# Front joined, side work reordered, and three products of the second scan made token-major and turned by TensorE

## The reference

```python
xs = _clamp(_layernorm(xs, norm_w, norm_b))
xz = xs @ in_proj_w.T
xin, z = jnp.split(xz, 2, axis=-1)
xc = silu(conv4(xin) + conv_b)               # 4 taps along the tokens
dt = softplus(xc @ x_proj_dt @ dt_proj_w.T + dt_proj_b); B, C = xc @ x_proj_bc
h = exp(dt * A) * h + (dt * x) * B           # 16 states, one step per token
y = einsum(h, C) + xc * D
out = layernorm(clamp((y * silu(z)) @ out_proj_w.T))
```

## Time and profile before

| | us |
|---|---|
| Median of 3 runs (203.24 to 204.24) | 203.94 |
| The profiled execution | 204.56 |
| Its span, first to last instruction | 202.8 |
| Around the span | 1.76 |

### The profile page before, as it was taken

The page is one execution under the profiler, slowest core; times in us unless marked ns, Lnnn a source line. Parts: engine busy times, 40 slices in busy tenths (PEclk is TensorE's granted clock), DMA queues, the critical chain, the costliest instruction groups (busy, mean ns, idle before and its releaser), DMA issues. The chain is left out here.

```text
span 202.8 us, 3714 instructions
## 1 busy us (share of the span) xinstructions
PE 178.0 (88%) x1194; PEld 149.2 (74%) x1194; DVE 135.2 (67%) x316; ACT 122.5 (60%) x281; POOL 106.5 (53%) x140
## 2 busy tenths in 40 slices
PE   6999858996887377799989999999989999999993
PEld 5678644643253124489979999899989999999992
DVE  2485999999899869998663727581377573333333
ACT  2717998999563636336658566767554655555530
POOL 4500044679796688689483445544466344344400
PEclk9999999999999969999999999999999999999999
DMA  5960299998450000000000000000000000000000
GB/s 148 327 194 0 36 389 353 326 306 255 170 216 36 0 0 0 0 0 3 2 0 3 2 0 3 0 0 3 0 2 0 3 2 0 22 9 3 0 0 26
DMA packets 7234, 14.38 MB, mean 71 GB/s; under 512 B 513, under 2 KB 3113, under 8 KB 6961
## 3 DMA queue, kind: packets, MB, share of 16 engines
q1 hardware_dynamic: 7216, 14.17, 21.8%
HBM read 13.88 MB, written 0.29 MB: 70 GB/s over the span
## 5 line engine op out<-in xcount | busy, mean ns | idle before, releaser
L933 DVE SCALAR_TENSOR_TENSOR acc<-dbx_ps,comb,acc 128x128 f32<-128x128 f32 x96 | 28.9, 344 | 30.8 <-PE dbx_ps L1211 30.5
L345 POOL TENSOR_TENSOR hc<-hs,cb 128x1024 f32<-128x1024 f32 x15 | 35.4, 2357 | 24.5 <-DMA cb<-c_rows 12.5
L1183 PE MATMUL bc_ps<-x_hi,w_hi 128*128 128x256 f32 x128 | 41.6, 325 | 0.8 <-DVE dbx_ps L767 0.8
L618 ACT ACTIVATE hid<-bc_ps,par 128x256 f32<-128x256 f32 x64 | 26.8, 471 | 21.9 <-PE bc_ps L1185 21.7
L363 POOL TENSOR_TENSOR w_lo<-w1b,w_hi 128x256 fp32r<-128x256 f32 x32 | 23.5, 735 | 27.4 <-ACT w_hi L610 27.2
L777 DVE TENSOR_TENSOR_SCAN hs<-da,dbx_ps 128x1024 f32<-128x1024 f32 x16 | 36.4, 2278 | 0.1
L1185 PE MATMUL bc_ps<-x_hi,w_lo 128*128 128x256 f32 x128 | 36.1, 282 | 0.0
L1184 PE MATMUL bc_ps<-x_lo,w_hi 128*128 128x256 f32 x128 | 35.9, 280 | 0.0
L1211 PE MATMUL dbx_ps<-w2b,hid 128*128 128x128 f32 (+1 forms) x256 | 33.9, 277 | 0.8 <-DVE acc L933 0.8
L1211 PE MATMUL dbx_ps<-w2a,hid 128*128 128x128 f32 x256 | 34.1, 276 | 0.3 <-ACT hid L618 0.2
L621 ACT ACTIVATE hid<-bc_ps 128x512 f32<-128x512 f32 x32 | 19.1, 597 | 24.0 <-PE bc_ps L1185 23.9
(11 more groups left out here) (183 smaller groups left out, 233.7 us busy)
## 6 DMA issues: line engine op xcount, KB each, us to landing
w1a<-w_in SPq DMA_DIRECT2D x2, 1024.0 KB, 9.1
cb<-c_rows SPq DMA_DIRECT2D x2, 1024.0 KB, 6.3
w1b<-w_in SPq DMA_DIRECT2D x2, 1024.0 KB, 14.4
cb<-c_rows SPq DMA_DIRECT2D x2, 768.0 KB, 5.4
cb<-taps_in SPq DMA_DIRECT2D x1, 512.0 KB, 5.1
cb<-c_rows SPq DMA_DIRECT2D x2, 256.0 KB, 3.9
par<-packed_in SPq DMA_DIRECT2D x1, 473.0 KB, 4.0
x_cm<-x_in SPq DMA_DIRECT2D x2, 128.0 KB, 2.1
```

Of the source, the lines that this page charges most:

```text
L345: nc.gpsimd.tensor_tensor(hc[p][:], hs[p][:], cb[:, k].rearrange("p i (o t) -> p i o t", o=1).to_broadcast([128, PAIR, DC, T]), ALU.mult). ...
L618: ins = nc.scalar.activation(hid[p][:, c, :], h_ps[p][:, T * c:T * (c + 1)], ACT.Gelu, bias=par[:, bass.ds(u * UC + at, 1)])
L933: nc.vector.scalar_tensor_tensor(acc[k][:, t, :], o_ps[:, w // span % RING, 128 * t:128 * (t + 1)], comb[layer][b][:, t, bass.ds(u, 1)], a ...
L1183: nc.tensor.matmul(h_ps[p][:, T * c:T * (c + 1)], w1_hi[w][:, at], x_hi[b][:], start=True, stop=False)
```

## The change

It has four parts.

1. The front. The taps are read from SBUF, without the ScalarE copies, and made in halves; ScalarE's copy of x comes ahead of its other work; TensorE's idle products are 256 wide and wait for nothing but their operands.
2. Softplus. One table set holds both Exp and Ln, so the loads around Ln go; the logarithm of 1 that this table gives is subtracted. ScalarE copies the C rows and B columns of batch 0, which VectorE did; GpSimd takes two subtractions of batch 0. For batch 1 ScalarE makes 1+e and VectorE is left with one instruction of two.
3. Side work. `step_x` follows `step_1` on GpSimd; the four high parts of the weights come between the scans, the low parts one by one; GpSimd does root_3 ahead of `hc` of m = 9.
4. Products. For m = 11, 13 and 15 (TURNED) VectorE's product goes. TensorE turns dt*x of batch 1 to token-major once (`turn`), ScalarE copies it to SBUF and scales it per token by a column of B (`token_products`, four instructions a pair), and TensorE turns the result into `dbx` (`turned_product`, eight transposes a pair). The `spread_b` of these pairs goes too.

```diff
...
+TURNED = (NP + 3, NP + 5, NP + 7)
...
+        dbx_tok = [sb(f"dbx_tok_{p}", [128, PAIR, TT, DI]) for p in range(RING)]
...
+        plan = [("constants",), ("x_stats", 0), ("x_stats", 1), ("x_norm", 0), ("rows_out",),
+                ("inner_x", 0), ("taps", 0, 0), ("in_proj", 0), ("taps", 0, 1), ("taps", 1), ("x_norm", 1), ("conv", 0), ("conv", 1), ("v", 0),
                 ("inner_x", 1), ("in_proj", 1), ("v_end",), ("bc", 0), ("softplus", 0), ("first_rows",), ("conv1", 0),
...
         b1_in = {3: [("silu1",)], 5: [("softplus", 1), ("bc_copy", 1)]}
-        b1_out = {1: [("z", 1)], 2: [("v", 1)], 3: [("bc", 1)], 4: [("rounding",), ("step_1",)], 5: [("step_x",)]}
+        b1_out = {1: [("z", 1)], 2: [("v", 1)], 3: [("bc", 1)], 4: [("rounding",), ("step_1",), ("step_x",)]}
         for k in range(NP):
             plan += [("pair_in", 0, k)] + b1_in.get(k, []) + [("pair_out", 0, k)] + b1_out.get(k, [])
+            if k == NP - 2:
+                plan += [("stage_lo", 0)]
+        plan += [("stage", u) for u in range(STAGED)]
         for k in range(NP):
             plan += [("pair_in", 1, k)] + [(name, 0, 0) for name in before_states.get(k, [])]
-            if k in (0, 2):
-                plan += [("stage", k), ("stage", k + 1)]
+            if k == 0:
+                plan += [("stage_lo", 1), ("stage_lo", 2)]
+            if k == 1:
+                plan += [("stage_lo", 3)]
+            if k in (0, 1, 3):
+                plan += [("tokens", TURNED[min(k, 2)])]
             if k == NP - 1:
                 plan += [("experts", 0, 0, 0, 1), ("bias2", 0, 0), ("experts", 0, 0, 1, 2)]
             plan += [("pair_out", 1, k)] + [(name, 0, 0) for name in after_states.get(k, [])]
...
+                for c in range(DC):
+                    low, e = dt_a[0][:, c], dt_e[0][:, c]
+                    pool.wait_ge(s["one_e"], c + 1)
+                    nc.gpsimd.tensor_tensor(low, e, low, ALU.subtract).then_inc(s["low_done"], 1)
...
+            def in_time(work):
+                at, root = work.index(("pair_out", 1, 1)), work.index(("root_3", 0, 0))
+                return work[:at] + [work[root]] + work[at:root] + work[root + 1:]
+            for step, *arg in in_time(plan):
...
                 act.wait_ge(s["ident_ready"], 1)
                 for c in range(DC):
                     ins = nc.scalar.activation(diag_d[:, c, :], ident[:], ACT.Identity, scale=col("d_skip")[:, c:c + 1])
@@ -459,10 +491,7 @@
             def rows_out():
                 act.wait_ge(s["wv_ps"], 1)
                 nc.scalar.activation(w_dt[:], halves(wv_ps), ACT.Copy).then_inc(s["wv_ready"], 1)
-            def taps_in(c):
-                act.wait_ge(s["taps_loaded"], 16)
-                nc.scalar.activation(taps_ps[c], taps_sb[:, c, :], ACT.Copy).then_inc(s["taps_ps"], 1)
+                skip_rows()
...
-                    nc.scalar.preload_act_table_set("exp_and_others")
+                    nc.scalar.preload_act_table_set("natural_log_exp_and_others")
...
-                    nc.scalar.preload_act_table_set("natural_log")
+                        if c == 0:
+                            act.wait_ge(s["ones_ready"], 1)
+                            nc.scalar.activation(ln_one[:], ones[:, 0:1], ACT.Ln).then_inc(s["ln_one_ready"], 1)
                     for c in range(DC):
                         act.wait_ge(s["exp_dt"], c + 1)
                         nc.scalar.activation(dt_l[0][:, c], dt_e[0][:, c], ACT.Ln, bias=ones[:, 0:1]).then_inc(s["ln_dt"], 1)
-                    nc.scalar.preload_act_table_set("exp_and_others")
+                        if c == 0:
+                            act.wait_ge(s["bct_ps"], 1)
+                            nc.scalar.activation(c_row[:, 0, :], bct_ps[0][0:NS, T:2 * T], ACT.Copy).then_inc(s["c_row_ready"], 1)
+                    act.wait_ge(s["ln_one_ready"], 1)
+                    nc.scalar.activation(ln_neg[:], ln_one[:], ACT.Copy, scale=-1.0).then_inc(s["ln_neg_ready"], 1)
+                    nc.scalar.activation(b_tok[:, 0], bct_ps[0][:, 0:TT * NS].rearrange("p (t r) -> p t r", t=TT),
+                                         ACT.Copy).then_inc(s["bct_ready"], 1)
...
-                nc.scalar.preload_act_table_set("natural_log")
                 act.wait_ge(s["exp_dt"], DC + 1)
-                nc.scalar.activation(dt_l[1][:], dt_e[1][:], ACT.Ln, bias=ones[:, 0:1]).then_inc(s["ln_dt"], 1)
-                nc.scalar.preload_act_table_set("exp_and_others")
+                nc.scalar.activation(halves(f_ps), dt_e[1][:], ACT.Identity, bias=ones[:, 0:1]).then_inc(s["one_e1"], 1)
+                nc.scalar.activation(dt_a[1][:], dt_e[1][:], ACT.Ln, bias=ones[:, 0:1]).then_inc(s["ln_raw"], 1)
+                act.wait_ge(s["ln_raw"], 1)
+                act.wait_ge(s["ln_neg_ready"], 1)
+                nc.scalar.activation(dt_l[1][:], dt_a[1][:], ACT.Identity, bias=ln_neg[:, 0:1]).then_inc(s["ln_dt"], 1)
...
+            def token_products(m):
+                j = TURNED.index(m)
+                if j >= RING:
+                    act.wait_ge(s["dbx_pe"], j - RING + 1)
+                for i in range(PAIR):
+                    for t in range(TT):
+                        n = PAIR * (m % NP) + i
+                        ins = nc.scalar.activation(dbx_tok[j % RING][:, i, t, :], dtx_tok[:, t, :], ACT.Identity,
+                                                   scale=b_tok[:, m // NP, t, n:n + 1])
+                ins.then_inc(s["dbx_tok_ready"], 1)
             def pair_in(b, k):
                 for j in (range(AHEAD) if b and k == 0 else (k + AHEAD - 1,) if b else (k,)):
                     if j < NP:
                         decays(b, j, (j + NP * b) % AHEAD)
+                if (b, k) == (1, 0):
+                    act.wait_ge(s["turn_ps"], 1)
+                    nc.scalar.activation(dtx_tok, f_ps.rearrange("p (t d) -> p t d", t=TT), ACT.Copy).then_inc(s["turned"], 1)
+                    act.wait_ge(s["turned"], 1)
...
-            def taps(c):
...
-                dve.wait_ge(s["taps_ps"], c + 1)
+                dve.wait_ge(s["taps_loaded"], 16)
+                at = slice(0, TAPS) if half is None else slice(TAPS // 2 * half, TAPS // 2 * (half + 1))
                 w_in = col("in_w")[:, 128 * c:128 * (c + 1)].rearrange("p (o d) -> p o d", o=1)
-                nc.vector.tensor_tensor(w_tap[:, c], w_in.to_broadcast([C, TAPS, 128]),
-                                        taps_ps[c].rearrange("p (k d) -> p k d", k=TAPS), ALU.mult).then_inc(s["taps_ready"], 1)
+                nc.vector.tensor_tensor(w_tap[:, c, at], w_in.to_broadcast([C, at.stop - at.start, 128]),
+                                        taps_sb[:, c, :].rearrange("p (k d) -> p k d", k=TAPS)[:, at], ALU.mult).then_inc(s["taps_ready"], 1)
...
-                    g, low, e = dt_q[0][:, c], dt_a[0][:, c], dt_e[0][:, c]
                     dve.wait_ge(s["abs_done"], c + 1)
-                    nc.vector.tensor_scalar(g, dt0_ps[c][:, 0:T], col("dt_b")[:, c:c + 1], 0.0, ALU.add, ALU.max).then_inc(s["r_done"], 1)
+                    nc.vector.tensor_scalar(dt_q[0][:, c], dt0_ps[c][:, 0:T], col("dt_b")[:, c:c + 1], 0.0, ALU.add,
+                                            ALU.max).then_inc(s["r_done"], 1)
                     dve.wait_ge(s["exp_dt"], c + 1)
-                    dve.wait_ge(s["r_done"], c + 1)
-                    nc.vector.tensor_tensor(g, g, e, ALU.add)
-                    link(nc.vector.tensor_scalar(low, e, 1.0, 1.0, ALU.add, ALU.subtract))
-                    link(nc.vector.tensor_tensor(g, g, low, ALU.subtract))
-                    if c == 0:
-                        bc_copy()
+                    nc.vector.tensor_scalar(dt_a[0][:, c], dt_e[0][:, c], 1.0, 1.0, ALU.add, ALU.subtract).then_inc(s["one_e"], 1)
                 for c in range(DC):
-                    dve.wait_ge(s["ln_dt"], c + 1)
-                    nc.vector.tensor_tensor(dt[:, c, 0, :], dt_q[0][:, c], dt_l[0][:, c], ALU.add).then_inc(s["dt0_ready"], 1)
+                    with_log(c)
+                    with_low(c)
...
-                dve.wait_ge(s["exp_dt"], DC + 1)
-                dve.wait_ge(s["relu_done"], 1)
-                link(nc.vector.tensor_scalar(halves(f_ps), dt_e[1][:], 1.0, 1.0, ALU.add, ALU.subtract))
-                nc.vector.tensor_tensor(dt_q[1][:], halves(f_ps), dt_e[1][:], ALU.subtract).then_inc(s["rounded"], 1)
+                dve.wait_ge(s["one_e1"], 1)
+                nc.vector.scalar_tensor_tensor(dt_q[1][:], halves(f_ps), 1.0, dt_e[1][:],
+                                               ALU.subtract, ALU.subtract).then_inc(s["rounded"], 1)
...
+                if m in TURNED:
+                    dve.wait_ge(s["dbx_pe"], TURNED.index(m) + 1)
+                else:
+                    dve.wait_ge(s["dbx_done"], made(m) + (1 + RING))
...
-                if 1 < m < NB * NP:
+                if 1 < m < NB * NP and m not in TURNED:
                     inputs(m // NP, m % NP, m % RING)
...
```

(47 more changed lines are left out.)

53 lines of the change are left out of this document (30 added, 23 removed).

## The result

| | before | after |
|---|---|---|
| Median of 10 runs each, one chip | 204.86 (203.24 to 206.23) | 202.62 (201.93 to 203.29) |
| Profiled execution | 204.56 | 202.17 |
| Its span | 202.8 | 200.4 |

The ratio is 0.990 (95% interval 0.9867 to 0.9933): 1.0% or 2.0 us faster, where I forecast 3.4 of 203.94 us, 1.7%. The profiles differ by 2.4 us.

What follows compares the result with a forecast made beforehand. VectorE was taken to set the time to about 87 us, TensorE from the experts' first output on. Gains 1.1+0.85+0.95-0.65+1.75-1.0+0.4 = 3.4 bring the median from 203.94 to 200.5 us; range 198.6 to 202.7.

Steps and rivals of the forecast that it cites:

- no low granted clock past 76: Sign from TensorE: the forecast would be wrong if its granted clock was low past 76 us.
- no idle time before gate_out: Sign between the scans: VectorE was forecast to stand idle 0.7 us before gate_out, waiting for its y sum.
- Front up to Abs: Start of the kernel to Abs: x copied first and a faster convolution gain 1.1 us, 0.75 if the clock is late.
- Softplus: Batch 0, Abs to first product: no table loads around Ln and work moved off VectorE gain 0.85 us.
- First scan: First scan stretch: one rounding instruction fewer and no wait for dt*x, less a late hc, gain 0.95 us.
- Between the scans: Stretch up to gate_out: GpSimd's low part makes hc of m = 7 late, costing 0.65 us.
- rival (d): Second scan: TensorE's clock stays low from 60 to 84 us, 7 us lost, 207.5 us in all; chance 0.06.
- Up to inner_norm: Second scan to inner_norm: product of m = 11 goes, GpSimd's chain rules; lead grows to 4.0, a gain of 1.75 us.
- tokens ahead of xg_tok: Up to the logits: ScalarE's four products for m = 15 stand ahead of xg_tok and cost 1.0 us.
- First output: Logits to the experts' first output: product of m = 15 goes, gaining 0.4 us; output at 84.0.
- The tail "unchanged": After the first output: the 64 units are unchanged, so the tail keeps its length, within 0.5 us.
- Rival (b): Products of m = 11, 13, 15: the turned ones gain nothing; total gain 1.9 to 2.2, 201.9 us; chance 0.14.

Runs made afterwards that it cites:

- filled: The changed kernel with idle products cut to TensorE's four longest idle times: 200.87 us, ratio 0.9825 to the kernel before.
- tokens_early: filled with ScalarE's scalings for m = 15 one pair earlier and one idle product instead of three ahead of to_channel: 199.92 us, ratio 0.9756.
- own_first: The changed kernel with VectorE's own_part (hc of m = 15) ahead of start_sum: 202.83 us, ratio 0.989; its profiled execution took 204.65.
- no_turn: The changed kernel without its fourth part, so VectorE makes the products of m = 11, 13 and 15 as before: 201.98 us, ratio 0.9852.
- before_filled: The kernel before the change with idle products put in TensorE's idle times: 205.71 us, ratio 1.0042.

## Why the prediction was right or wrong

The direction held, and so did these marks: no idle time before the product of m = 8, 1.26 before L900 (forecast 1.3), 2.24 before logit_max (over 2), no low granted clock past 76. Missed: no idle time before gate_out, first output at 84.58 instead of 84.0, a longer tail. The time I forecast was 2.1 us too low (202.62 lies at the edge of my 198.6 to 202.7): 1.2 by the gain (3.4 against 2.2 between the medians), 0.9 because the kernel before stood that much higher in these runs. Term by term, forecast and measured in the profile:

- Front up to Abs 1.1, measured 1.72 (18.60 to 16.88): the convolution came down to 3.72 entirely. Softplus 0.85, measured 0.57 (5.94 to 5.37): the first of VectorE's joined instructions (19.13) took 1.05, the second 0.48. GpSimd's second subtraction ran beside the first, where I had both ended before VectorE asks; that it is the cause is not tested. Together 2.28 for 1.95.
- First scan 0.95, measured 0.93 at scan 7.
- **Between the scans -0.65, measured -1.6: the step that failed.** I worked this stage out from GpSimd's queue alone, priced the late hc of m = 5 as 0.25 on scan 7, and did not follow TensorE's queue: an idle time of 2.79, the clock low behind it, and the B rows of m = 9 in line behind the slow y sum. `filled` shows the term without the clock: gate_out's lead is 2.96, the loss 0.25. My rival (d) had the mechanism but looked for it only behind the y sum of m = 10. In this profile the y sums of m = 9 and 10 ran low too (5.34 for 8 records from 66.10), with nobody waiting: gate_out to L900 is 12.94, as in tokens_early. Behind them the clock stayed up here and fell in own_first's profile, with 1.8 more up to the first output.
- Up to inner_norm +1.75, measured 1.64. Right; by no_turn the turned products have no part in it.
- tokens ahead of xg_tok -1.0, measured -0.85 at xg_tok and -0.83 at logit_max. Right.
- First output +0.4, measured 0.40.
- The tail "unchanged", measured -0.4. Scan 15 ends earlier against GpSimd's queue, which changes who goes first at the shared ports. I took "the 64 units are unchanged" to mean that their time is unchanged too.

1.95 + 0.95 - 0.65 + 1.75 - 1.0 + 0.4 = 3.4 (forecast); 2.28 + 0.93 - 1.6 + 1.64 - 0.83 + 0.4 - 0.4 = 2.4 (measured). With the clock kept, `filled` stands 3.5 of span below before_filled (3.8 below the kernel before) and at a ratio of 0.9825: my sum was one for a TensorE that keeps its clock. That it fits so well is part luck, for the front (+0.3), this stage (+0.4) and the tail (-0.35) were each off. Rival (b), that the three products gain nothing, came closest to the time and is right in its statement: from gate_out on they cost about 1.0 net where they were put (142.4 against 141.4). Shown by runs: clock, order, tokens. The tail's cause is argued from the rows of four profiles (pair 2.87 or 3.33); the run made for it gave nothing back, so it stays open in part.
